# A four-layer graph network: eight-head probabilities normalised before their transposes, logits tiles of 128 columns, and a new order of steps

## The reference

```
h = relu(norm(x)); x = x + L0(h)   # 4-head attention, elu, 1-head attention, elu, FFN, layer norm
h = relu(norm(x)); x = x + L1(h)   # 8-head scaled dot-product attention, masked by adj
h = relu(norm(x)); x = x + L2(h)   # deg * (h Wi + b) + adj (h Wj)
h = relu(norm(x)); x = x + L3(h)   # 1-head attention; [attention output, h W]
```

```
scores = q k^T / sqrt(32), masked; p = exp(scores - max); attn = p / sum(p)
out = attn v (heads side by side) @ Wo.T + bo
```

## Time and profile before

| | us |
|---|---|
| median of 3 runs | 2894.32 |
| lowest, highest | 2891.27, 2897.72 |
| profiled execution, its own time | 2894.04 |
| its span | 2892.3 |
| PE (matmuls) busy in it | 2739.9 (95%) |
| DVE busy | 2289.1 (79%) |
| ACT busy | 2282.5 (79%) |
| POOL busy | 1778.2 (61%) |

### The profile page before, as it was taken

How to read it: one execution, slowest core, us unless ns; L and a number is a source line. 1 busy time by engine, 2 the same in 40 slices (tenths; PEclk the granted TensorE clock), 3 DMA queues, 4 the chain that set the end, 5 groups by cost and what they waited for, 6 DMA issues and landing times.

```text
span 2892.3 us, 74656 instructions
## 1 busy us (share of the span) xinstructions
PE 2739.9 (95%) x23809; PEld 2489.8 (86%) x23809; DVE 2289.1 (79%) x9428; ACT 2282.5 (79%) x7175; POOL 1778.2 (61%) x4510
## 2 busy tenths in 40 slices
PE   2899999999999999999999999999999999999985
PEld 2798888888888888988888988988888888888884
DVE  4688888888888888888888888888888888888874
ACT  2788888888888878878888888888888888888773
POOL 2566666666666666666666666666666666666652
PEclk9999999999999999999999999999999999999996
DMA  3000000000000000000000000000000000000000
GB/s 106 1 12 16 13 14 15 13 14 15 13 15 14 12 16 13 13 16 13 13 16 13 12 16 13 13 16 13 13 16 13 14 14 13 15 14 13 14 7 8
DMA packets 43398, 44.96 MB, mean 16 GB/s; under 512 B 4864, under 2 KB 42496, under 8 KB 42880
## 3 DMA queue, kind: packets, MB, share of 16 engines
q1 hardware_dynamic: 41280, 37.96, 4.2%
q10 hardware_dynamic: 1728, 2.23, 0.3%
HBM read 23.40 MB, written 16.78 MB: 14 GB/s over the span
## 4 chain that ended last, share of the span: by engine, by line
PE 93%; DVE 3%; issue 2%; ACT 1%; SPq 1%; POOL 0%; DMA 0%; DVEq 0%; POOLq 0%
PE pB L960 13%; PE pA L885 12%; PE pB L945 9%; PE pB L996 8%; PE pE L885 6%; PE pF L870 5%; PE pC L996 4%; PE pC L885 3%; PE pF L885 3%; PE pB L885 3%; PE pA L870 3%; PE pC L986 3%; PE pF L1053 3%; PE pA L1034 2%; PE pE L1072 2%; PE pE L875 2%
## 5 line engine op out<-in xcount | busy, mean ns | idle before, releaser
L576 ACT ACTIVATE F_s_t<-F_s_t,F_m 128x128 f32<-128x128 f32 x1024 | 327.6, 404 | 0.0
L960 PE MATMUL pB<-wout_high,B_h_high 128*128 128x258 f32 x1024 | 325.7, 318 | 1.5 <-POOL B_h_low L395 1.5
L960 PE MATMUL pB<-wout_high,B_h_low 128*128 128x258 f32 x1024 | 290.1, 283 | 0.0
L960 PE MATMUL pB<-wout_low,B_h_high 128*128 128x258 f32 x1024 | 289.0, 282 | 0.0
L945 PE MATMUL pB<-attnT,whs 128*128 128x128 f32 x2048 | 285.2, 282 | 0.7 <-ACT attnT L506 0.7
L945 PEld LDWEIGHTS pB<-attnT,whs 128*128 128x128 f32 x2048 | 250.3, 193 | 16.2 <-ACT attnT L506 1.1
L960 PEld LDWEIGHTS pB<-wout_high,B_h_high 128*128 128x128 f32 x1024 | 193.8, 189 | 25.4 <-issue 21.2
L885 PE MATMUL pA<-wh_high,A_hT_high 128*128 128x512 f32 x512 | 211.5, 413 | 0.0
L568 ACT ACTIVATE D_q_t<-pB,bq_c 128x128 f32<-128x128 f32 x256 | 80.1, 364 | 161.9 <-PE pB L996 161.9
L499 ACT ACTIVATE A_l<-A_l,A_m 128x128 f32<-128x128 f32 x512 | 198.2, 396 | 3.8 <-DVE A_m L701 3.8
L885 PE MATMUL pA<-wh_low,A_hT_high 128*128 128x512 f32 x512 | 200.8, 392 | 0.0
(11 more groups left out here) (241 smaller groups left out, 11374.2 us busy)
## 6 DMA issues: line engine op xcount, KB each, us to landing
xs<-in_x SPq DMA_DIRECT2D x128, 128.0 KB, 2.0
out_x<-xs SPq DMA_DIRECT2D x128, 128.0 KB, 1.7
a_b<-in_a_heads ACTq DMA_DIRECT2D x1, 1024.0 KB, 5.4
wh_w<-in_w_heads SPq DMA_DIRECT2D x2, 512.0 KB, 8.0
wout_w<-in_w_out SPq DMA_DIRECT2D x1, 1024.0 KB, 6.7
w_w<-in_w SPq DMA_DIRECT2D x2, 256.0 KB, 12.1
wij_w<-in_wijT SPq DMA_DIRECT2D x1, 512.0 KB, 7.2
aout_b<-in_a_out ACTq DMA_DIRECT2D x1, 256.0 KB, 12.0
```

The costliest lines, as they stand in the source:

```text
L576: last = act.activation(F_s[:, h, :], F_s[:, h, :], ACT.Exp, scale=-1.0, bias=F_m[:, h:h + 1])
L960: last = pe.matmul(pB[:, 0, 0:D + 2], a, w[:, k, :], start=(k == 0 and i == 0), stop=(k == KH - 1 and i == 2))
```

## The change

The eight-head probabilities are divided by their sums in SBUF, four heads at a time, before they are transposed: F_recip becomes F_recip.0 and F_recip, F_norm.0 and F_norm multiply 128x512 elements in place, and F_rb, F_rT, F_rTc and F_on are gone. F_pT.0 and F_pT wait for F_norm.0 and F_norm. F_high follows F_o directly. F_sum.0 and F_sum take contiguous halves. C_f3 and E_f3 become 128 columns wide, zeroed once, so C_fT and E_fT write 128 partitions (their copies still take 6). All four orders are laid anew. The semaphore names and the tiles F_rb and F_rT are left out of the diff below.

```diff
--- before.py
+++ after.py
...
@@ -31,21 +31,21 @@
-C_fT C_s F_s B_o.0 A_zT C_pT E_ah C_o A_f B_o E_m F_pT.0 A_wh_hi A_wh_lo E_zT3 C_hT A_fT F_pT E_h C_hid D_zT A_s
-B_wh.0 F_rT F_o E_fT B_wh.1 E_s C_ffn D_k.0 D_kv B_wh.2 B_wh E_pT F_out E_o D_q A_pT
+C_fT B_o.0 C_s F_s A_zT C_pT E_ah C_o A_f B_o E_m C_hT A_wh_hi D_zT C_hid A_wh_lo A_fT F_pT.0 E_zT3 D_k.0 E_h F_pT
+A_s C_ffn D_kv E_fT B_wh.0 F_o E_s B_wh.1 B_wh.2 B_wh E_pT F_out E_o A_pT D_q
-C_leaky E_high C_exp C_attn A_hT E_ahhigh A_high F_exp.0 B_neg A_fc C_oexp B_exp B_neg.0 F_pTc.0 F_exp B_exp.0
-A_whc_hi E_hT3 C_hTc B_high.0 A_whc_lo E_hc F_pTc C_hidc D_hT C_high D_high A_leaky B_high E_leaky F_high A_exp D_kc
-E_exp E_attn B_whc D_qc A_attn
+C_leaky E_high C_exp C_attn A_hT E_ahhigh C_oexp A_high F_exp.0 B_neg A_fc B_exp B_neg.0 C_hTc F_exp D_hT B_exp.0
+A_whc_hi D_high C_hidc C_high E_hT3 B_high.0 A_whc_lo E_hc B_high A_leaky F_pTc.0 F_pTc A_exp F_high E_leaky D_kc
+E_exp E_attn B_whc A_attn D_qc
-E_stats E_moments A_stats C_fTc A_moments D_stats E_z C_max A_z E_low D_moments C_recip F_max.0 E_ahlow F_max
-F_sum.0 E_x3 D_z E_stats3 E_moments3 C_min B_h C_h E_z3 B_h.0 F_sum A_fTc B_low.0 F_recip F_rb F_rTc E_fTc F_on
-A_max C_y C_stats E_max C_moments F_low C_g A_recip D_vc E_recip A_norm C_x1 F_x2 E_left
+E_stats E_moments A_stats C_fTc A_moments D_stats E_z C_max D_moments A_z E_low F_max.0 C_recip E_ahlow C_min D_z
+C_h F_max F_sum.0 B_h E_x3 E_stats3 F_recip.0 E_moments3 F_norm.0 F_sum F_recip E_z3 F_norm B_h.0 A_fTc B_low.0
+A_max C_y E_fTc C_stats C_moments C_g F_low E_max A_recip A_norm D_vc E_recip C_x1 F_x2 E_left
-C_fcopy E_rstd A_rstd D_rstd E_xb A_low A_fcopy E_rstd3 C_hb C_xb E_fcopy C_low D_low B_low D_xb C_rstd E_right
+C_fcopy E_rstd A_rstd D_rstd E_xb A_low C_hb C_xb A_fcopy E_rstd3 D_low C_low E_fcopy E_right B_low D_xb C_rstd
...
@@ -163,7 +163,7 @@
-        C_f3, C_frest, C_fT = sb("C_f3", [P, 3 * 2], BF16), sb("C_frest_t", [P, 2]), sb("C_fT_t", [P, P], BF16)
+        C_f3, C_frest, C_fT = sb("C_f3", [P, P], BF16), sb("C_frest_t", [P, 2]), sb("C_fT_t", [P, P], BF16)
...
@@ -188,7 +187,7 @@
-        E_f3, E_frest, E_fT = sb("E_f3", [P, 3 * 2], BF16), sb("E_frest_t", [P, 2]), sb("E_fT_t", [P, P], BF16)
+        E_f3, E_frest, E_fT = sb("E_f3", [P, P], BF16), sb("E_frest_t", [P, 2]), sb("E_fT_t", [P, P], BF16)
...
@@ -275,7 +274,7 @@
-        ZEROED, BUILT = 11, 22
+        ZEROED, BUILT = 13, 24
...
@@ -330,7 +329,8 @@
-            pool.memset(A_f3[:, :], 0.0).then_inc(consts_built, 1)
+            for t in (A_f3, C_f3, E_f3):
+                pool.memset(t[:, :], 0.0).then_inc(consts_built, 1)
...
@@ -600,7 +600,7 @@
-                "F_high": copy("F_on", "F_high", F_hl[0][:, :], pF[:, 0, 0:D]),
+                "F_high": copy("F_o", "F_high", F_hl[0][:, :], pF[:, 0, 0:D]),
...
@@ -780,31 +780,27 @@
-                    pairs = slice(c * HPC // K, (c + 1) * HPC // K)
-                    total = F_sum[:, :].rearrange("p (c j) -> p j c", c=K)[:, pairs, :]
-                    p = F_s[:, :, :].rearrange("p (j c) m -> p j c m", c=K)[:, pairs, :, :]
-                    dve.tensor_reduce(total, p, AX.X, ALU.add).then_inc(S["F_sum" if c == K - 1 else "F_sum0"], 1)
-                return step
-            def F_recip(g):
-                done(dve, "F_sum", g)
-                dve.reciprocal(F_rec[:, :], F_sum[:, :]).then_inc(S["F_recip"], 1)
-            def F_rb_step(g):
-                done(dve, "F_recip", g)
-                done_before(dve, "F_rT", g)
-                dve.tensor_copy(F_rb[:, :].rearrange("p (h d) -> p h d", d=DH),
-                                F_rec[:, :].unsqueeze(2).to_broadcast([P, HEADS_L1, DH])).then_inc(S["F_rb"], 1)
-            def F_rTc(g):
-                done(dve, "F_rT", g)
-                dve.tensor_copy(F_rT[:, :], pF[:, 1, 0:D]).then_inc(S["F_rTc"], 1)
-            def F_on(g):
-                done(dve, "F_o", g)
-                done(dve, "F_rTc", g)
-                dve.tensor_tensor(pF[:, 0, 0:D], pF[:, 0, 0:D], F_rT[:, :], ALU.mult).then_inc(S["F_on"], 1)
+                    half = slice(c * HPC, (c + 1) * HPC)
+                    dve.tensor_reduce(F_sum[:, half], F_s[:, half, :], AX.X, ALU.add).then_inc(S["F_sum" if c == K - 1 else "F_sum0"], 1)
+                return step
+            def F_recip(c):
+                def step(g):
+                    done(dve, "F_sum" if c == K - 1 else "F_sum0", g)
+                    half = slice(c * HPC, (c + 1) * HPC)
+                    dve.reciprocal(F_rec[:, half], F_sum[:, half]).then_inc(S["F_recip" if c == K - 1 else "F_recip0"], 1)
+                return step
+            def F_norm(c):
+                def step(g):
+                    done(dve, "F_recip" if c == K - 1 else "F_recip0", g)
+                    half = slice(c * HPC, (c + 1) * HPC)
+                    dve.tensor_tensor(F_s[:, half, :], F_s[:, half, :],
+                                      F_rec[:, half].unsqueeze(2).to_broadcast([P, HPC, P]), ALU.mult)\
+                       .then_inc(S["F_norm" if c == K - 1 else "F_norm0"], 1)
+                return step
...
@@ -843,7 +839,8 @@
-                "F_max": F_max(1), "F_sum.0": F_sum_step(0), "F_sum": F_sum_step(1), "F_recip": F_recip, "F_rb": F_rb_step, "F_rTc": F_rTc, "F_on": F_on,
+                "F_max": F_max(1), "F_sum.0": F_sum_step(0), "F_sum": F_sum_step(1), "F_recip.0": F_recip(0), "F_recip": F_recip(1),
+                "F_norm.0": F_norm(0), "F_norm": F_norm(1),
...
@@ -1037,7 +1034,7 @@
             def F_pT_step(c):
                 def step(g):
-                    done(pe, "F_exp" if c == K - 1 else "F_exp0", g)
+                    done(pe, "F_norm" if c == K - 1 else "F_norm0", g)
                     done(pe, "F_max", g)
...
@@ -1054,11 +1051,6 @@
-            def F_rT_step(g):
-                done(pe, "F_rb", g)
-                done(pe, "F_pTc", g)
-                transposes(pF[:, 1, :], F_rb, K).then_inc(S["F_rT"], 1)
...
@@ -1111,7 +1103,7 @@
-                "F_pT.0": F_pT_step(0), "F_pT": F_pT_step(1), "F_o": F_o_step, "F_rT": F_rT_step,
+                "F_pT.0": F_pT_step(0), "F_pT": F_pT_step(1), "F_o": F_o_step,
```

More of the change, by code:

```diff
@@ L58 @@
 D_stats D_moments D_var D_rstd D_z D_xb D_zT D_hT D_high D_low D_kv D_kc D_vc D_q D_qc
-F_s F_max0 F_max F_exp0 F_exp F_pT0 F_pT F_pTc0 F_pTc F_o F_sum0 F_sum F_recip F_rb F_rT F_rTc F_on F_high F_low F_out F_x2
+F_s F_max0 F_max F_exp0 F_exp F_pT0 F_pT F_pTc0 F_pTc F_o F_sum0 F_sum F_recip0 F_recip F_norm0 F_norm F_high F_low F_out F_x2
 E_stats E_moments E_var E_rstd E_z E_high E_low E_xb E_ah E_ahhigh E_ahlow E_m E_x3 E_stats3 E_moments3
@@ L182, in gnn_stack @@
         F_m, F_sum, F_rec = (sb(n, [P, HEADS_L1]) for n in ("F_m", "F_sum_t", "F_rec"))
-        F_rb, F_rT = sb("F_rb_t", [P, D]), sb("F_rT_t", [P, D])
         F_hl = high_low("F_oT", [P, D])
```

## The result

The changed kernel takes 2945.03 us (median of 4 runs, 2944.39 to 2947.89) against 2894.73 before. The ratio is 1.0176, 95% interval 1.0162 to 1.0189. It is 1.8% slower, where 2843 us and a gain was forecast. Nearly all of it lies in the rounds: from the first D_z to the last of the 128 it is 2888.1 - 98.5 = 2789.6 us, against 2837.7 - 95.4 = 2742.3 before, so a mean of 21.97 us a round against 21.59 (127 rounds each).

What follows compares the result with a forecast made beforehand. PE, busy 95% of the span, was taken as the bound. Gains of 0.22 + 0.18 = 0.40 us a round over 128 rounds, 51 us, took 2894.04 to 2843 us; range 2806 to 2880.

Steps and rivals of the forecast that it cites:

- part 4: DVE and ACT: new F_norm work adds some 0.4 us busy time on DVE, stays under the round; PE loses nothing.
- the room of 0.15 us at A_s: Behind F_norm, B_h.0, its high part, A_whc_lo and A_s follow; the least room found there was 0.15 us.
- The sum for PE: PE's round: 0.22 us from F_rT plus 0.18 from A_pT to A_zT, 0.40 a round, giving 2843 us.
- A_zT's start: PE: A_zT starts 1.45 us after C_s, behind C_max and A_z on DVE; PE arrives at 1.06, waits 0.39.
- The part of the sum taken from F_rT: Part 1, PE: removing F_rT's two instructions before F_o gains 0.22 us a round, 0.31 at most.
- The slower rival: DVE between F_sum.0 and B_h.0: F_norm takes 1.290 us, delaying B_h.0 and A_s 1.03 us a round; 2975 us, chance 0.10.
- The second-wait rival: ACT or DVE 0.4 us later than laid out, A_s having 0.15 room: PE loses 0.25 a round; 2875 us, chance 0.15.
- The wide tile: Rival: bf16, not width, costs the extra time; 0.09 us returns, 2855; with exposed loads 2868. Chance 0.10, half with loads.
- Part 2: PE from A_pT to A_zT, reordered with wide C_fT: 2.93 us without D_q, a gain of 0.18 a round.
- "I take 0" for E_fT: Part 3, PE: moving wide E_fT from behind F_o to between D_kv and B_wh.0 gains 0, 0.1 us either way.
- F_norm hidden: DVE: two F_norm at 0.698 us each stay under the round and end before F_pT.0 and F_pT need them.
- The signs named in advance: PE rounds 21.1 to 21.3 us, no C_s wait, A_zT waiting some 0.3, F_norm near 0.70; wrong if PE waits at A_s.

Runs made afterwards that it cites:

- the kernel with three waits: Changed kernel (the two engines kept apart) plus three GpSimd waits: A_low for D_z, D_low for E_z3, D_xb for C_g; 2840.78 us, ratio 0.9816 to before.
- One wait on the engine that has time: Changed kernel plus only the GpSimd wait of A_low for D_z; 2842.54 us, ratio 0.9821 to the kernel before.

## Why the prediction was wrong

- **The step that failed** is part 4, "The vector engines", and in it the lay-out of DVE's order by the durations of before. "It stays under the round" is true and was not the question. Each operation was given the length that it had beside the old neighbours on POOL. D_z and E_z got 0.4 us and took 0.85 and 0.92, which made PE wait 0.75 us a round in three places; with the two engines kept apart the time fell by 104 us. So the room of 0.15 us at A_s, and the larger room at E_zT3 and D_zT, was gone. The new POOL and DVE orders were never laid side by side in time.
- **The sum for PE was right, its terms in the main.** 0.40 us a round and 2843 us were forecast for a kernel in which DVE works as before; with the two engines kept apart 2840.78 us was measured. The round is 21.16 against 21.18, A_zT's start behind C_s 1.46 against 1.45. The wait in it is 0.53 where 0.39 was forecast, since C_s and F_s take less room than the 1.06 us that was taken for them; the chain over DVE sets A_zT's start, so that error cost nothing. The part of the sum taken from F_rT was not tried alone.
- **The slower rival** had the right place, DVE ahead of B_h.0 and then A_s, and the right chain, but the wrong cause: F_norm ran at 0.67 us, below its 0.698. What ran long were the D_z and E_z beside it. POOL working beside DVE was named there, and its price was not sought for any other operation. At 2975 it was also the only rival above the range. The second-wait rival named 0.25 us a round from A_s alone, where three waits came to 0.75. Neither named D_zT or E_zT3.
- **The wide tile** does what it says: the extra time belongs to the narrow tile and not to bf16. Part 2 had 0.09 us for C_fT; in the new order two narrow tiles cost 0.4, and in the old one the gain is eaten. (In that rival, 25 us on top of the 0.09 us of the first case gives 2880; 2868 is 25 us on the forecast alone.) "I take 0" for E_fT was right for a wide tile; a narrow one in E_fT's new place would have cost about half of the 0.40.
- **F_norm hidden**: right, with the qualification that its length shifts E_z.
- **The signs named in advance** held in part: no wait at C_s, a wait at A_zT (0.53 us, and not some 0.3), F_norm near 0.70. The round was 21.97 us and not 21.1 to 21.3. "It would be wrong if PE waits at A_s" is what the profile showed.

## What to carry to other kernels

When the orders of VectorE and GpSimd change, lay both in time and look at each pair that overlaps: a tensor_scalar or an operation with two SBUF inputs on one side, an SBUF read on the other. Here the VectorE operation that was held ended 0.15 or 0.28 us after GpSimd's, whatever room the busy shares showed. Not every overlap costs: F_sum (L784), a sum over one input, took 0.68 us beside C_xb as it did before the change, and C_y, with one input in PSUM, 0.42 beside B_low. One wait on the engine that has time bought 102 us. And a chain of in-order lists that is right on paper should be checked against the lengths in its own trace, not in that of its predecessor.

## What was not expected of the hardware

- A DVE tensor_scalar of 128x256 beside a GpSimd subtract of 128x256 ended 0.15 to 0.16 us after it in three pairs, two of which began within 0.04 us of each other. In one of these DVE had begun first (E_z at 1509.32, D_low at 1509.36).
- C_g, with two SBUF inputs, was held as well, 0.81 against 0.48 us, and ended 0.28 us after D_xb.
- It goes both ways, and then GpSimd's end keeps its distance to VectorE's. C_hid_low on POOL, 0.73 us in the kernel before, took 1.11 us from 1510.32 in the changed kernel, beside an F_norm that had started at 1510.16; it ended 0.59 us after F_norm. D_low beside F_norm in the kernel with three waits (1.05 us) and C_hb beside E_z in the kernel before (0.83 us) also ended 0.59 us after the VectorE operation.
- Even a 128x1 operation on GpSimd is held: E_ve, 0.19 us in the kernel before, took 0.54 beside F_norm.0.
